# Attention over gathered rows: in every fourth chunk the last of four gathers is replaced by a one-hot matmul lookup, its 21 matmuls laid over four periods, and one wait of the gather queue is gone

## The reference

```python
x = _layernorm(x + _L0_gnn_ref(x, edge_attr3_2x64, src, dst), axis=-1)
...
Q = jnp.einsum('nf,hfd->hnd', x, Wq)
K = jnp.einsum('nf,hfd->hnd', x, Wk)
V = jnp.einsum('nf,hfd->hnd', x, Wv)
s = jnp.einsum('hef,hef->eh', Q[:, receiver], K[:, sender]) * scale
m = jax.ops.segment_max(s, receiver, num_segments=n)
p = jnp.exp(s - m[receiver])
alpha = p / jax.ops.segment_sum(p, receiver, num_segments=n)[receiver]
out = nan_to_num(segment_sum(alpha * V[:, sender], receiver).mean(heads))
x = _layernorm(x + (x + out @ Wout), axis=-1)
```

## Time and profile before

| | us |
|---|---|
| median of 3 runs | 2564.44 (2561.57 to 2565.7) |
| the profiled execution, its own time | 2559.61 |
| its span | 2557.9 |
| PE busy | 2040.9 (80%) |
| PE weight loads busy | 1508.0 (59%) |
| DVE busy | 1727.1 (68%) |
| ACT busy | 1313.3 (51%) |
| POOL busy | 1881.4 (74%) |

### The profile page before, as it was taken

One profiled execution on the slowest core, in us unless ns is written; L12 is line 12 of the kernel. 1 busy time (PEld: TensorE's weight loads), 2 busy tenths in 40 slices (PEclk: granted clock), 3 DMA queues, 4 the chain that ended last, 5 costly groups with the idle time before them and its releaser, 6 DMA issues.

```text
span 2557.9 us, 75060 instructions
## 1 busy us (share of the span) xinstructions
PE 2040.9 (80%) x18960; PEld 1508.0 (59%) x18961; DVE 1727.1 (68%) x5572; ACT 1313.3 (51%) x3792; POOL 1881.4 (74%) x2347
## 2 busy tenths in 40 slices
PE   3999999878778877777887887787787878777886
PEld 3888888845555555545555555554565555554555
DVE  7999999786565555555665565555555666665567
ACT  5555555365454544544545545545545455554544
POOL 2888888777677777777777777777777777777750
PEclk9999999677576666677766667767757676777678
DMA  5787787312121212212122121221221212222111
GB/s 157 252 257 251 256 256 251 68 35 45 34 46 38 46 37 46 46 38 46 38 45 46 37 46 38 46 45 39 45 45 38 47 37 46 41 42 46 37 22 27
DMA packets 187098, 195.56 MB, mean 76 GB/s; under 512 B 106955, under 2 KB 109851, under 8 KB 184729
## 3 DMA queue, kind: packets, MB, share of 16 engines
q1 hardware_dynamic: 137278, 139.69, 19.7%
q0 software_dynamic: 49312, 50.59, 10.6%
HBM read 184.89 MB, written 5.25 MB: 74 GB/s over the span
## 4 chain that ended last, share of the span: by engine, by line
POOL 45%; PE 27%; issue 18%; DVE 4%; DMA 4%; ACT 1%; DVEq 0%; ACTq 0%; POOLq 0%; SPq 0%
POOL XS L632 43%; PE psVX L1376 4%; PE psN L1385 4%; PE psM L1385 4%; PE psS L1559 3%; DMA XS<-x_dram,dst_bs 3%; PE psVX L1514 2%; PE psM L1514 2%; PE psT L1509 1%; PE psA L1370 1%; PE psVX L1504 1%; PE psA L1524 1%; PE psA L1514 1%; PE psA L1450 1%; PE psS L1450 1%
## 5 line engine op out<-in xcount | busy, mean ns | idle before, releaser
L632 POOL DMA_INDIRECT XS<-x_dram,dst_bs x1516 | 1447.3, 955 | 473.3 <-issue 447.6
L926 DVE SCALAR_TENSOR_TENSOR l_st<-l_st,alpha,rsum 64x1 f32 x782 | 169.4, 217 | 515.8 <-PE psM L1514 268.1
L1559 PE MATMUL psS<-XT,Ubuf 96*128 96x512 f32 x522 | 416.3, 893 | 16.6 <-ACT Ubuf L1231 15.9
L1280 ACT COPY PmPT<-psT 128x512 f32<-128x512 f32 x196 | 114.9, 586 | 336.8 <-PE psT L1509 336.0
L998 DVE TENSOR_REDUCE rmax<-psS 128x1 f32<-128x512 f32 x391 | 270.5, 692 | 20.1 <-PE psS L1559 5.1
L1514 PEld LDWEIGHTS psVX<-XS,PmPT 128*128 128x128 f32 x1568 | 280.2, 267 | 1.6 <-ACT PmPT L1280 1.3
L1514 PE MATMUL psVX<-XS,PmPT 128*128 128x64 f32 x1568 | 279.7, 342 | 0.7 <-ACT PmPT L1280 0.7
L1504 PEld LDWEIGHTS psN<-ident,XS 128*128 128x128 f32 x366 | 55.2, 183 | 379.7 <-issue 379.2
L1504 PEld LDWEIGHTS psVX<-ident,XS 128*128 128x128 f32 x392 | 59.4, 183 | 365.7 <-issue 364.7
L1280 ACT COPY dst_bs<-psT 128x512 f32<-128x512 f32 x195 | 114.3, 586 | 301.2 <-PE psT L1509 300.2
L1514 PEld LDWEIGHTS psM<-XS,dst_bs 128*128 128x128 f32 x1464 | 262.4, 267 | 1.6 <-ACT dst_bs L1280 1.6
(11 more groups left out here) (286 smaller groups left out, 4220.8 us busy)
## 6 DMA issues: line engine op xcount, KB each, us to landing
big<-in_edge_attr_2x SPq DMA_DIRECT2D x342, 256.0 KB, 3.3
row_pair<-x_dram SPq DMA_DIRECT2D x2944, 0.2 KB
big<-dst_turned SPq DMA_DIRECT2D x49, 512.0 KB
XS<-x_dram,dst_bs POOLq DMA_INDIRECT x1516, 2.5
O<-in_edge_attr_2x SPq DMA_DIRECT2D x48, 256.0 KB, 3.3
O<-codes_dram SPq DMA_DIRECT2D x200, 6.0 KB
x_dram<-x SPq DMA_DIRECT2D x12, 128.0 KB, 2.0
out<-big SPq DMA_DIRECT2D x12, 128.0 KB
```

Source lines behind the costliest of these rows:

```text
L632: pool.indirect_dma_start(row_block(c, j), None, x1_dram, bass.IndirectOffsetOnAxis(ap=idx2[b % SB][:, k * CPP + j:k * CPP + j + 1], axis= ...
L926: dve.scalar_tensor_tensor(out=ls, in0=ls, scalar=al[half], in1=rs[half], op0=ALU.mult, op1=ALU.add)
L1280: act.copy(PTs[a][:, :], psT[:, :]).then_inc(pt_done, 1)
L1559: pe.matmul(psSc[1 - a][:, :], Ubuf[1 - a][:, :], XT[(J - 1) % 3][:, :], start=True, stop=True).then_inc(s_done, 1)
```

## The change

In 95 chunks (12, 16, 20, ... 388, `looked_up`) the fourth block is not gathered but looked up from x1 in SBUF. A source node n is n = 128 h + p; its row is in partition p of x1's block h (49 blocks), and h is split as 7 s + l. The lookup has these parts:

- In the written-out periods x1 is split into three bf16 parts (`parts`, which takes x1's place in SBUF), with two copies by ACT and two subtractions by DVE of 128 x 448 for each of 7 pieces. DVE makes for all looked-up edges a code 128 s + p and the number l; SP stores the codes to `code_dram`. PE turns the l's (one transpose, `psA`).
- For each lookup r, SP broadcasts 128 codes to all partitions (`load_code`, 64 KB, into two halves of tile `A`). DVE compares them with 7 x 128 constants, which gives 7 one-hot 128 x 128 matrices in bf16 (`look_hot`, ahead of period 7 + 4r).
- PE multiplies them with the parts: 21 matmuls of 128 x 448, bf16, all into `psA` (`look`), 4 of them in the first period of the four, then 6, 6 and 5, in three places of a period: ahead of the turning of rows, ahead of the turning of probabilities, ahead of the scores.
- DVE picks the l-th of 7 groups of 64 (`look_pick`: one masked product over 448 columns and one reduction) and writes the block into its slot of XS. PE waits for that (`looked`) two periods later.

The rest of the change: POOL's wait for `s_done` ahead of the third gather is gone. Further visits use the bank `psXc[J % 2]` instead of `psA`, for which PE waits for `u_done` first and for `x_upd` at the end of each visit. `centre_x1` is gone: DVE keeps only the means, x1 is loaded again from `x1_dram` after the last lookup, and POOL adds the means in 13 instructions ahead of clearing `aggT`. SP loads row ids 16 at a time and issues 32 rows after each of two codes where it issued 64 in one go. The scratch for dynamic DMA descriptors goes from 8192 to 4096 bytes.

```diff
-        return sum(CPP - 1 if by_row(k) and k != RC0 else CPP for k in range(c % S2, c + 1, S2))
+        return sum(blocks_gathered(k) for k in range(c % S2, c + 1, S2))
...
+    LP = ((0, 4), (4, 6), (6, 8), (8, 10), (10, 12), (12, 14), (14, 16), (16, 18), (18, 21))
...
+            def load_code(r, more):
+                row = code_dram[r:r + 1, :] if isinstance(more, int) else code_dram[bass.ds(more * LPI + r, 1), :]
+                sp.dma_start(code_b[r % 2], row.broadcast_to([P, P])).then_inc(l_code[r % 2], 16)
...
                 load_dst_of(b, more)
-                if b // 2 < RN:
-                    load_rows_of(b // 2, b % 2, more)
+                for k, r in enumerate(codes_behind(b)):
+                    sp.wait_ge(l_hot, r - 1 + more * LPI)
+                    load_code(r, more)
+                    if b // 2 < RN:
+                        load_rows_of(b // 2, (b % 2 * 2 + k, b % 2 * 2 + k + 1), more)
...
+            sp.wait_ge(l_sum, LN)
+            sp.dma_start(x1v[:, :, :], x1_dram.rearrange("(b p) d -> p b d", p=P)).then_inc(s_lcst, 16)
...
-                for j in range(CPP - 1 if by_row(c) and c != RC0 else CPP):
-                    if j == CPP // 2 and c >= S2:
-                        pool.wait_ge(s_done, c - S2 + 6)
+                for j in range(blocks_gathered(c)):
                     pool.indirect_dma_start(row_block(c, j), None, x1_dram,
                                             bass.IndirectOffsetOnAxis(ap=idx2[b % SB][:, k * CPP + j:k * CPP + j + 1], axis=0)).then_inc(xg[k], 16)
 
+            pool.wait_ge(s_lcode, 1)
+            pool.wait_ge(s_lcst, 32)
+            for g in range(TG):
+                b0, nb = TB * g, blocks(g)
...
-                        dve.tensor_reduce(rmaxX[:, :], psA[:, :], AX_X, ALU.max).then_inc(x_max, 1)
+                        dve.tensor_reduce(rmaxX[:, :], psF[:, :], AX_X, ALU.max).then_inc(x_max, 1)
...
+                if i is not None and (J - H2) % LE == LE - 1:
+                    look_pick(J, i)
...
+            def part_of(k):
+                if k > 0:
+                    dve.wait_ge(s_tmid, k)
+                    dve.tensor_tensor(parts[:, k - 1, 2, :], hot_pick[:, :], parts[:, k - 1, 1, :], ALU.subtract).then_inc(s_tlo, 1)
+                    dve.wait_ge(s_tlo, k)
+                if k < LG:
+                    dve.wait_ge(s_thi, k + 1)
+                    dve.tensor_tensor(hot_pick[:, :], x1[:, k * LW:(k + 1) * LW], parts[:, k, 0, :], ALU.subtract).then_inc(s_trest, 1)
...
+            def look_hot(J, i):
+                r = (J - H2) // LE
+                q = r % 2
+                dve.wait_ge(l_code[q], 16 * (r // 2 + 1) + i * (8 * LPI))
+                dve.wait_ge(looked, r + 1 + i * LPI)
+                dve.tensor_tensor(hot.rearrange("p (s e) -> p s e", s=LG), code_b[q].unsqueeze(1).broadcast_to([P, LG, P]),
+                                  code_of.unsqueeze(2).broadcast_to([P, LG, P]), ALU.is_equal).then_inc(l_hot, 1)
+
+            def look_pick(J, i):
+                r = (J - H2) // LE
+                dve.wait_ge(l_sum, r + 1 + i * LPI)
+                dve.scalar_tensor_tensor(out=hot_pick[:, :], in0=lane_of, scalar=lane_col[:, bass.ds(i * LPI + r, 1)], in1=psL,
+                                         op0=ALU.is_equal, op1=ALU.mult).then_inc(l_pick, 1)
+                dve.wait_ge(l_pick, r + 1 + i * LPI)
+                dve.tensor_reduce(xs((LC0 + r * LE) % S2, CPP - 1), hot_pick[:, :].rearrange("p (l f) -> p f l", f=D), AX_X, ALU.add).then_inc(looked, 1)
...
+            def look(J, i, place):
+                t = 3 * ((J - H2) % LE) + place - 2
+                if i is None or not 0 <= t < len(LP):
+                    return
+                first, end = LP[t]
+                if first == 0:
+                    pe.wait_ge(s_tlo, LG)
+                    pe.wait_ge(l_hot, (J - H2) // LE + 1 + i * LPI)
+                for n in range(first, end):
+                    last = pe.matmul(psL, hot[:, n // 3 * P:(n // 3 + 1) * P], parts[:, n // 3, n % 3, :], start=(n == 0), stop=(n == 3 * LG - 1))
+                if end == 3 * LG:
+                    last.then_inc(l_sum, 1)
...
+                        pe.wait_ge(u_done, taken)
...
+                        pe.wait_ge(x_upd, pe.snap(xv, min_val=2))
...
+                look(J, i, 0)
...
+                    if i is not None and (J - LC0) % LE == 0:
+                        pe.wait_ge(looked, (J - LC0) // LE + 2 + i * LPI)
                     pe.sem_inc(turn_steps, 1)
                     turn_rows(J, a)
                 if on(4):
                     pe.wait_ge(pt_done, vv)
                     weigh(J - 4, PTs[a], psVc[a][:, 0:D], pv_done)
+                look(J, i, 1)
                 if on(3):
                     pe.wait_ge(exp_done, vv)
                     turn_probs(Pms[1 - a], psT, tp_done)
-                    further_visits(J - 3)
+                    further_visits(J - 3, vv)
+                look(J, i, 2)
                 if on(1):
```

151 lines of the change are left out of this document (122 added, 29 removed).

## The result

| | before | after |
|---|---|---|
| median of the runs | 2564.88 us (4 runs) | **2522.72 us** (4 runs, 2516.69 to 2528.36) |
| the profiled execution, its own time | 2559.61 | 2528.36 |
| its span | 2557.9 | 2525.7 |
| granted clock of the whole span | 0.743 | 0.885 |

The ratio is 0.984 (0.9826 to 0.9854): faster, clear of the noise, but by 1.6% where the prediction had 3.7%, and the time lies outside its range (2443 to 2515). It falls in the range of rival 2, "PE bound in part" (2525), whose mechanism is at most a part of it, as is shown at the end.

The account below looks back on a forecast made before the run. POOL's gathers were taken to set the attention's pace, PE just keeping up. Terms -118.8 + 5 + 4 + 2 + 14 - 1 + 1 = -94 us from 2564.4 gave 2469 us, own range 2455 to 2490, stated range 2443 to 2515.

Parts of the forecast that it names:

- rival 2: PE bound in part, half-clock share f of 0.1 to 0.25 or matmuls nearer 0.23 us: 2525 us (2490 to 2560), chance 0.14.
- The gathers: On POOL, 95 gathers go at 1.25 us each, -118.8 us; the 1446 left stay 1.25 us apart.
- rival 3: DVE's one-hot comparison holds POOL's gathers up: 2575 us if each blocks fully, 2520 if half; chance 0.04.
- PE's matmuls and clock: 21 matmuls of 0.20 us a lookup at full clock; PE's period 4.2 us against POOL's 4.62, granted clock above 0.9.
- DVE: Comparison, pick and reduction take 2.3 us in four periods; DVE does not bound, late exponential costs PE 0 to 0.2 us a period.
- PE falling behind: PE's lag beyond POOL's lead, taken as 19 us, eats gain: start +5, visit pair +4, other visits +2, end +14.
- The first pair: Further visits at 668 and 687 us put PE 13 us over POOL's lead, where 8.6 were lost before: +4 us.
- Of the others: Of the other further visits, two or three come too close for PE's recovery of 0.4 us a period: +2 (0 to +8).
- The end: Two visits in the loop's last 60 us leave PE 12 to 15 us more behind its rows: +14 (+5 to +20).
- The removed wait: POOL's dropped wait for scores lets two gathers out near the visit pair: -1 us (-5 to 0).
- SP and the tail: SP's 36 of 37 us a block fits: 0; x1's reload and POOL's mean additions finish in time: 0 (0 to +10).
- Rival 1: PE keeps its half-clock stretches and becomes the bound, so slower: 2655 us at f = 0.40, chance 0.09.

Follow-up runs that it names:

- the kernel with both moves: Changed kernel with first lookup matmuls one place back on PE, and DVE's pick and reduction behind the running maximum: 2503.1 us, 0.9763 to the kernel before.
- one place too far: Changed kernel with first lookup matmuls one place back, pick and reduction behind the mask, comparison behind the first period's mask: 2743.6 us, 1.0697 to the kernel before.

## Why the prediction was wrong, step by step

**The gathers.** 95 x 1.25 held for what was taken away (119.7 us). That the others keep their pace did not: 1.2700 us instead of 1.2596, +15 us. I had rival 3 for this, with 106 or 45 us, and gave it 0.04, by a single gather that kept 0.94 us. The kernel without lookups is at 1.2646 and the one with the comparisons alone at 1.2738: by these the comparison makes 8 us (up to 1.2700) to 13 us. The 7 us from 1.2596 to 1.2646, with no comparison in the loop, stay unexplained; the smaller descriptor scratch and SP's new order of issue were not tried by themselves. One row beside one instruction was too little; the means of all gathers that overlap it would have been needed. The Trainium skill (SBUF — State Buffer, Who interferes with whom) has a DVE instruction with two SBUF inputs contend with a GpSimd instruction that reads SBUF, and infers that descriptor generation is spared. The gather of 1.81 us beside such an instruction agrees with the first half and speaks against sparing the gather as a whole; which of its steps is held up no run shows.

**PE's matmuls and clock.** Right in size for the matmuls: they follow one another in 0.19 us at full clock (two take 0.54 us, three 0.73), where I took 0.20. But PE catches up at 4.45 us a period instead of 4.2, so that against 4.65 it makes up 0.2 us a period, half of my 0.4. Without visits it never stops POOL for over 1 us. The clock came to 0.86 to 0.90 in the loop, just short of the "above 0.9". The Trainium skill (TensorE: Matmul & The Clock Gate, HAM oscillation) has gaps bring the half clock; with it agree the cycle above, where the half clock follows two waits of 1.20 and 0.79 us, and the kernel with both moves, where these waits fell from 153 to 55 us and the clock rose to 0.912.

**DVE.** The reduction takes 920 ns and not 550 to 650, so comparison, pick and reduction are 2.7 us, not 2.3. Worse was "0 to 0.2 us a period, within my 4.2". I saw that the exponential comes late, and let PE's two or three lookup matmuls cover it. But in that very period the only lookup matmuls are those that wait for DVE's comparison. The two waits cost 85.5 + 67.8 us of PE, and half clock after them. On the chip both moves together brought 20 us.

**PE falling behind: the step that failed.** The first pair was to lose 9 us more than before, and did: its stops are 5.9 and 12.3 us where it was 8.6. "Of the others, two or three come too close for a recovery of 0.4: **+2**" is the term that failed: it measured 45 us. The cost of a visit was about right: 10.5 us were put down, and a visit's period less the pace of 4.65 gives 9.8 to 15.5 us, 10.6 in the median. The lead was not. "Now PE was two visits, 18 to 19 us, behind. I take 19 us as what POOL's lead covers": but at that point POOL had already stopped for 8.58 us. What the row says is 19 less 8.6, **about 10 us**, and one visit uses all of it. The trace of the changed kernel agrees: where PE is not behind, the weighing of chunk c-8 ends 11.4 us (median) before the first gather of chunk c, for which POOL must wait for it. Then each visit costs about what PE was behind ahead of it, and five of the nine others find PE 4 us or more behind. Two errors meet here, and the ledger itself can weigh them, as an estimate for the seven visits between the first pair and the last two: with the prediction's lead of 19 and 0.4 us made up a period they stop POOL for 3 us, with a lead of 10 for 17, with 0.2 us made up as well for 32, and with the visits' measured lengths for 39; measured are 48. Nine of the 11 stop POOL; the last two come when it is nearly done, and make the end late. That the visits are what costs is shown by the kernels without them (75 us against 20); that the lead is nearer 10 than 19, by the one with a chunk's lead less (+26, where 19 would have left 0 to 10). And the wait at a visit's end I had put in, with "four DVE steps of 0.2 to 0.3 us", but not asked where it is needed: moved, it gave 16 to 23 us.

**The end** was +14 and measured +18.6. **The removed wait**: -3 to 9 us where I had 1. **SP and the tail**: 0, as forecast; from the last update to the end it is 53.5 us, 54.3 before. The additions of the means take 7.17 us on POOL, within 5 to 11, and end 2.2 us ahead of the sums' first scaling.

**Rival 2** named the time and the symptom (PE binds in part), and its condition came true as well: 24% of the loop (600 to 2380 us) runs at half clock, where it had f at 0.1 to 0.25. The half clock is a part of why PE makes up only 0.2 us a period. But a PE that is the bound by its rate would not wait 87.5 us for rows, and without visits, with f still at 0.17, it stops POOL nowhere for over 1 us. So the clock as such is not the cause, and that the time comes out at the rival's 2525 is in part luck. Rival 1 is out.

Two figures of the prediction are slightly off by its own numbers, with no effect on the forecast: 1950 us over 391 chunks is 4.99 us and not 4.97, and rival 1's price at f = 0.63 comes to about 2875 and not 2850.

## What to carry to other kernels

When a lead (buffers ahead) hides rare stalls, work out its length as the stall less the stop that is seen, and then ask how far the consumer is behind when the next stall comes: a producer made faster shortens the lead in time and the pauses in which the consumer recovers. An engine may have room for added work in the mean and still lose, if what it must wait for falls into one period: place the pieces so that no two waits meet, and read who waits for whom before moving them, since one place too far cost about 220 us here. And a wait that guards a buffer belongs ahead of the next write to it, not behind the last use.
